# GpSimd takes up node work earlier in the program of a graph layer, and DVE and ACT share the output tiles differently until then

## The reference

```python
deg = jnp.maximum(jnp.zeros((n,), x.dtype).at[dst].add(1.0), 1.0)
edge_weight = (deg[src] * deg[dst]) ** (-DEG_POWER)
edge_msg = jax.nn.relu(edge_attr @ W1e + b1e) @ W2e + b2e
messages = (x[src] + edge_msg) * edge_weight[:, None]
agg = jax.ops.segment_sum(messages, dst, num_segments=n)
combined = (1.0 + gin_eps) * x + agg
h = jax.nn.relu(combined @ W1n + b1n) @ W2n + b2n
out = h + x
out = out * jax.lax.rsqrt(jnp.mean(out * out, axis=-1, keepdims=True) + RMS_EPS) * rms_w
x = _layernorm(x + out, axis=-1)
```

## Time and profile before

| | |
|---|---|
| median of 3 runs | 1333.68 us (1332.87 to 1334.81) |
| the profiled execution | 1332.28 us |
| its span in the profile | 1330.5 us |
| mean granted TensorE clock | 0.970 |
| DVE busy | 1260.0 us, 95% |
| PE busy | 1159.0 us, 87% |
| ACT busy | 1072.8 us, 81% |
| POOL busy | 971.8 us, 73% |

### The profile page before, as it was taken

How to read it: one execution, slowest core, us unless ns; L and a number is a source line. 1 busy time by engine, 2 the same in 40 slices (tenths; PEclk the granted TensorE clock), 3 DMA queues, 4 the chain that set the end, 5 groups by cost and what they waited for, 6 DMA issues and landing times. The chain is left out here.

```text
span 1330.5 us, 32120 instructions
## 1 busy us (share of the span) xinstructions
PE 1159.0 (87%) x7478; PEld 848.1 (64%) x7591; DVE 1260.0 (95%) x4743; ACT 1072.8 (81%) x3857; POOL 971.8 (73%) x1281
## 2 busy tenths in 40 slices
PE   4999729999999999998798888888888888899991
PEld 2555317777777777776576666666666666678771
DVE  5999988999999999999499999999999999899997
ACT  4999505666666666666589999999999999999996
POOL 7777744777777777677777777777777702599896
PEclk9999859999999999999799999999999999999996
DMA  4999964655555555776767888878777665677654
GB/s 123 396 352 396 389 242 111 181 165 171 173 178 177 162 176 172 247 246 249 279 228 260 303 306 298 325 285 306 297 283 282 240 226 196 238 273 278 255 209 184
DMA packets 87132, 327.93 MB, mean 246 GB/s; under 512 B 24657, under 2 KB 27456, under 8 KB 62556
## 3 DMA queue, kind: packets, MB, share of 16 engines
q1 hardware_dynamic: 55832, 256.51, 51.3%
q0 software_dynamic: 29904, 69.48, 17.1%
q10 hardware_dynamic: 1268, 0.54, 0.2%
HBM read 180.14 MB, written 153.95 MB: 251 GB/s over the span
## 5 line engine op out<-in xcount | busy, mean ns | idle before, releaser
L680 POOL DMA_INDIRECT xs<-in_x,src_x x392 | 385.9, 985 | 143.0 <-issue 119.0
L706 POOL DMA_INDIRECT agg_scratch<-staged,sca_i x385 | 381.1, 990 | 121.9 <-issue 113.3
L893 ACT ACTIVATE squares<-res 128x128 f32<-128x128 f32 x784 | 290.1, 604 | 0.5 <-DVE res L1217 0.5
L1433 PE MATMUL bank<-cT,w1n 128*128 128x512 f32 x392 | 215.8, 633 | 68.0 <-ACT cT L875 67.9
L893 ACT ACTIVATION_READ_ACCUMULATOR squares<-res 128x1 f32 x784 | 256.3, 496 | 0.0
L904 ACT ACTIVATE on<-z,offset,rstd 128x128 f32<-128x128 f32 x462 | 255.8, 846 | 0.4 <-DVE offset L1183 0.4
L1410 PEld LDWEIGHTS bank<-w2n,hn 128*128 128x128 f32 x1568 | 206.5, 192 | 70.4 <-issue 64.5
L1410 PE MATMUL bank<-w2n,hn 128*128 128x128 f32 x1568 | 207.3, 275 | 4.2 <-ACT hn L880 0.7
L880 ACT ACTIVATE hn<-bank,b1n_c 128x512 f32<-128x512 f32 x196 | 191.2, 975 | 3.5 <-PE bank L1433 3.5
L1339 PE MATMUL bank<-digits,picks 128*128 128x221 f16 x1568 | 185.2, 260 | 0.0
L875 ACT ACTIVATE cT<-bank 128x512 f32<-128x512 f32 x196 | 172.3, 879 | 8.6 <-PE bank L1426 8.6
(11 more groups left out here) (179 smaller groups left out, 2348.6 us busy)
## 6 DMA issues: line engine op xcount, KB each, us to landing
agg_scratch<-zeros SPq DMA_DIRECT2D x48, 1024.0 KB
xn<-in_x SPq DMA_DIRECT2D x48, 1024.0 KB
out<-on SPq DMA_DIRECT2D x48, 1024.0 KB, 4.5
ag<-agg_scratch SPq DMA_DIRECT2D x47, 1024.0 KB, 7.0
sums_scratch<-sums SPq DMA_DIRECT2D x49, 512.0 KB
staged<-sums_scratch POOLq DMA_DIRECT2D x28, 896.0 KB
highq<-src_key_scratch SPq DMA_DIRECT2D x49, 256.0 KB, 3.7
ea<-in_edge_attr SPq DMA_DIRECT2D x42, 256.0 KB
```

What stands on the lines that cost most here:

```text
L680: pool.indirect_dma_start(out=xs[:, b % XS, j, :], out_offset=None, in_=x, in_offset=bass.IndirectOffsetOnAxis(ap=src_x[:, t:t + 1], axis= ...
L706: pool.indirect_dma_start(out=agg_rows, out_offset=bass.IndirectOffsetOnAxis(ap=sca_i[:, t:t + 1], axis=0), in_=staged[:, k % STAGES, j, : ...
L893: last = act.activation(squares[:, j, :], res[:, s, j, :], ACT.Square, accum_out=ssq[:, v // SPB, s * TB + j:s * TB + j + 1])
L1433: pe.matmul(ps[2 + s][:, :], w1n[:, :], cT[:, s, :], start=True, stop=True).then_inc(hn_done, 1)
```

## The change

GpSimd makes the products from step 104 on (`MIX_ALONE`) and its output tiles from step 88 on (`END_ALONE`), both 128 before. Until step 88 DVE and ACT share the four output tiles 2:2 in even steps and 1:3 in odd ones (`first_ends`), 1:3 before. From step 88 on ACT has tile 3 alone. The written and looped parts move: DVE, ACT and PE now have 0 to 47 written, 48 to 95 looped, 96 to 111 written, 112 to 191 looped; GpSimd begins at 96. In GpSimd's list the output tiles of steps 88 to 91 (n = 106 to 109) stand before the first products, those of step 104 (n = 110).

```diff
-    ALONE = 128
-    assert ALONE % (SPB * XR) == 0 and ALONE <= SPLIT * SPB
+    MIX_ALONE, END_ALONE = 104, 88
+    assert MIX_ALONE <= SPLIT * SPB and END_ALONE <= SPLIT * SPB
...
-            rounds, alone = STEPS // unroll, ALONE // unroll
+            rounds = STEPS // unroll
+            first = min(MIX_ALONE + 6, END_ALONE + 16) // unroll
+            then = -(-max(MIX_ALONE + 7, END_ALONE + 20) // unroll)
...
-            if begin == 0 and alone > 3:
+            if alone_too:
                 written(0, 3 * unroll)
-                looped(3, alone)
-                written(ALONE, ALONE + 2 * unroll)
-            else:
-                written(begin, ALONE + 2 * unroll)
-            looped(alone + 2, rounds)
+                looped(3, first)
+            written(first * unroll, then * unroll)
+            looped(then, rounds)
             written(rounds * unroll, STEPS + tail)
...
+        def mixed_alone(m):
+
+            return below(m, MIX_ALONE)
+
+        def ended_alone(m):
+
+            return below(m, END_ALONE)
+
+        def first_ends(m, v):
+
+            return 2 - v % 2
...
-                if live(m, STEPS) and not solo(m):
+                if live(m, STEPS) and not mixed_alone(m):
                     _, xsl, _, h = place(m, u - 6)
...
-                    if solo(m):
+                    if ended_alone(m):
                         continue
-                    if isinstance(m, int) and m == ALONE:
-                        pool.wait_ge(fin_ready, ALONE)
+                    if isinstance(m, int) and m == END_ALONE:
+                        pool.wait_ge(fin_ready, END_ALONE)
...
-                    share = 3 if solo(m) else 1 if not isinstance(B, int) or B < SPLIT else 2 if B < BLOCKS - 2 else 1 if B < BLOCKS - 1 else 2 if m < STEPS - 1 else 0
+                    share = TB - first_ends(m, v) if ended_alone(m) else 1 if not isinstance(B, int) or B < SPLIT else 2 if B < BLOCKS - 2 else 1 if B < BLOCKS - 1 else 2 if m < STEPS - 1 else 0
...
-                if live(m, STEPS) and solo(m):
+                if live(m, STEPS) and mixed_alone(m):
...
-                if live(m, STEPS) and not solo(m):
-                    dve.wait_ge(xsc_ready, at(m + 1 - ALONE))
+                if live(m, STEPS) and not mixed_alone(m):
+                    dve.wait_ge(xsc_ready, at(m + 1 - MIX_ALONE))
...
-                if live(m, STEPS) and solo(m):
+                if live(m, STEPS) and ended_alone(m):
                     B, o, h = m // SPB, (v // SPB) % OR, (v % SPB) * TB
...
-                    dve.tensor_scalar(on[:, o, h, :], z[:, v, 0, :], neg_mean[:, v // SPB, h:h + 1],
-                                      rstd[:, v // SPB, h:h + 1], ALU.add, ALU.mult).then_inc(fin_ready, 1)
+                    for j in range(first_ends(m, v)):
+                        last = dve.tensor_scalar(on[:, o, h + j, :], z[:, v, j, :], neg_mean[:, v // SPB, h + j:h + j + 1],
+                                                 rstd[:, v // SPB, h + j:h + j + 1], ALU.add, ALU.mult)
+                    last.then_inc(fin_ready, 1)
```

More of the change, by code:

```diff
@@ L411, in run, with run_nodes @@
                 step(n, n % unroll)
-        def run_nodes(eng, step, tail, begin=0):
+        def run_nodes(eng, step, tail, alone_too=True):
             unroll = SPB * XR
-            rounds, alone = STEPS // unroll, ALONE // unroll
+            rounds = STEPS // unroll
+            first = min(MIX_ALONE + 6, END_ALONE + 16) // unroll
+            then = -(-max(MIX_ALONE + 7, END_ALONE + 20) // unroll)
             def written(lo, hi):
@@ L425, in looped, with below @@
                         step(Count(i, unroll, u, lo, hi), u)
-            if begin == 0 and alone > 3:
+            if alone_too:
                 written(0, 3 * unroll)
-                looped(3, alone)
-                written(ALONE, ALONE + 2 * unroll)
-            else:
-                written(begin, ALONE + 2 * unroll)
-            looped(alone + 2, rounds)
+                looped(3, first)
+            written(first * unroll, then * unroll)
+            looped(then, rounds)
             written(rounds * unroll, STEPS + tail)
-        def solo(m):
-            return m < ALONE if isinstance(m, int) else m.below(ALONE)
         def live(n, total):
             return not isinstance(n, int) or 0 <= n < total
+        def below(m, limit):
+            return m < limit if isinstance(m, int) else m.below(limit)
+        def mixed_alone(m):
[4 more added lines that the diff above has]
+            return 2 - v % 2
         def late(B):
@@ L773, in node_step @@
                         last.then_inc(fin_ready, 1)
-            run_nodes(pool, node_step, 15, ALONE)
+            run_nodes(pool, node_step, 15, alone_too=False)
         @block.scalar
```

## The result

The changed kernel takes 1350.13 us, median of 4 runs (1350.01 to 1350.47), against 1333.28 for the kernel before on the same chip: the ratio is 1.0129 (95% interval 1.0117 to 1.0142). It is slower, as forecast, by 17 us instead of 25. All four executions stand within 0.5 us.

The account below looks back on a forecast made before the run. ACT sets 3.616 us a step without GpSimd; mixed, all four engines are full; GpSimd's scatter queue delays the handover. Span 1330.5 + 53.1 - 28.4 = 1355.2, median 1358.4; own range 1349 to 1364, to 1369 with more holes.

Parts of the forecast that it names:

- z of step 104 starts: Handover on DVE: this z waits for GpSimd's scatters, join, output tiles and products, starting at 1079.5 instead of 1026.4, 53.1 us later.
- 88 mixed steps, bare: From the z of step 104 to that of step 192, all steps mixed at 2.832 us each: 249.2 us.
- hole at n=176: Idle stretch where DVE's 16-step loop returns in the mixed stage: 3.3 us, counted once as before, 9.9 more as bound.
- low clock after the wait: PE stands still some 45 us and restarts at the low clock level: 1.5 us lost, bounds 0 and 4.
- from the z of step 192 to the end: Tail of the kernel behind the 88 mixed steps: 21.8 us.
- span: Whole profiled execution: 1330.5 + 53.1 - 28.4 = 1355.2 us.
- GpSimd's release: Join starts 5.3 us after the last scatter, could give back up to 4; it lands in 2.0, bounds 0 and 4.5.
- Rival 2: Mixed loop on DVE: the hole at n=176 repeats at each return, + 9.9 us, 1368; chance 0.15.
- The share: Output tiles 1:3 and 2:2 before the handover: DVE bounds at 3.58 a step; free before the wait, otherwise about 2 us either way.
- Rival 1: Handover: GpSimd free by step 104, no wait worth the name, 18.8 us faster, median 1315; chance 0.04.
- Rival 4: Smaller wait: last scatters and join land at once, no holes, no clock loss, pace 2.809; about 1346; chance 0.05 below 1349.
- Rival 3: Up to step 88, DVE's 44 extra output tiles slow scatters; last one 15 us later, median 1373; chance 0.04.

Follow-up runs that it names:

- experiment 1: Changed kernel with two of every 14 scatters left out (336 instead of 385, output incomplete): 1295.78 us, ratio 0.9722 to the kernel before.
- experiment 5: Changed kernel with products from step 120 and output tiles from step 104, new share: 1314.13 us, ratio 0.9848 to the kernel before.
- experiment 8: Changed kernel with products from step 120 and output tiles from 104, old share 1:3: 1310.95 us, ratio 0.9832 to the kernel before.
- experiment 12: Changed kernel with three DVE output tiles a step and 172 one-column memsets ahead of DVE's node steps: 1355.01 us, ratio 1.0162 to the kernel before.
- experiment 2: Changed kernel with only the new share, GpSimd taking up products and output tiles at 128 as before: 1325.49 us, ratio 0.9942 to the kernel before.
- experiment 3: Changed kernel with products from step 104, output tiles from 128, old share 1:3: 1369.76 us, ratio 1.0276 to the kernel before.
- experiment 4: Changed kernel with products from step 128, output tiles from 88, old share 1:3: 1353.39 us, ratio 1.0153 to the kernel before.
- experiment 6: Changed kernel with products from step 116 and output tiles from step 100, new share: 1319.83 us, ratio 0.9903 to the kernel before.
- experiment 7: Changed kernel with products from step 124 and output tiles from step 108, new share: 1318.67 us, ratio 0.9895 to the kernel before.
- experiment 9: Changed kernel with three output tiles a step on DVE and one on ACT until step 88: 1377.20 us, ratio 1.0331 to the kernel before.
- experiment 10: Changed kernel with two output tiles a step on DVE and two on ACT until step 88: 1353.02 us, ratio 1.0152 to the kernel before.
- experiment 11: Changed kernel with 84 one-column memsets on DVE ahead of its node steps: 1377.91 us, ratio 1.0342 to the kernel before.

## Why the prediction was right

The mechanism held in each step: the change makes DVE wait at the z of step 104 for a GpSimd that is still scattering, and experiment 1 shows that this wait is the whole loss. The size, in span, by the terms of the sum (the terms of the first line add up to 1079.4, not 1079.5):

| term | forecast | measured | difference |
|---|---|---|---|
| z of step 104 starts | 1079.5 | 1076.73 | -2.8 |
| 88 mixed steps, bare | 249.2 | 249.7 | +0.5 |
| hole at n=176 | 3.3 | none | -3.3 |
| low clock after the wait | 1.5 | inside the 249.7, at most 0.5 | -1.5 |
| from the z of step 192 to the end | 21.8 | 21.9 | +0.1 |
| span | 1355.2 | 1348.3 | -6.9 |

The forecast of the median adds 1.4 us more, by which the profiled execution before stood under its median; here the two stand 0.1 us apart. So 1350.1 against 1358.4.

- *GpSimd's release.* The join follows the last scatter 2.08 us later instead of 5.30, since SP's store and loads no longer run beside it. I had named this and left it out of the value. The other runs bear it out, whether DVE waits or not: where SP issued its store and two loads within the 5.5 us up to the last scatter (the kernel before and experiments 1, 5, 8 and 12), the join follows after 5.30 to 6.73 us without work; where SP issued nothing in the 9 us before it (the changed kernel and experiments 2 to 4, 6, 7 and 9 to 11), after 2.08 or 2.09. Landing took 2.10 (I took 2.0).
- *The hole.* I carried the one of before over into a loop that had been moved. It doesn't come with the loop's return as such: the loop now returns four times without one, and in experiment 3, whose loop has the steps 160 to 191 as before but stands elsewhere in the list, the two steps at n=176 take 5.8 us (1276.40 to 1282.18) and not 9.0. In the kernel before, six packets of queue 14 fall between 1233 and 1246, and none between 1220 and 1233. This fits the stretches of experiments 9 and 11, but no run moved the loop of the kernel before alone, so that the hole is the same thing is not shown. Rival 2, which repeated it at each return, was wrong for this kernel; experiments 9 and 11 show that four stretches would have come, of 7 us each and not 3.3, had the loop stood 84 instructions further on. I had no grounds to exclude that, and 1378 lay outside my range: that the time fell inside it is in this respect luck.
- *The clock.* It was down to 0.51 during the wait, close to the lower level of 1.2 GHz, as foreseen. Behind the wait it stayed low for some 4 us: 0.50 from 1077 to 1079, 0.70 on average from 1078 to 1084, 1.00 from 1084 to 1090. So the low clock came as forecast, and only its price was too high: the first four steps behind the wait took 11.7 us (residuals at 1077.34 and 1089.02) against 11.3. The loss is at most half a us.
- *The share.* The pace without GpSimd is 14.33 us for four steps (residuals at 902.61 and 916.94), 3.58 each, as worked out. Alone the share is worth 7 us (experiment 2), not 2: most of what I missed lies between n=135 and n=150. In front of the wait it is worth nothing, as forecast.
- *Rival 1* (no wait) is refuted by the 51.85 us. *Rival 4* (a smaller wait, below 1349) was missed by 1.1 us, and three of its five terms came true: no hole, no loss by the clock worth the name, and 3.2 us less before the join. Its other two didn't: the join still took 2.10 us to land, and the pace was 2.837, not 2.809. *Rival 3* (DVE's tiles hold scatters back) is not seen in this kernel, whose last scatter is 0.45 us late, but see the last section.

## What to carry to other kernels

Before work is moved earlier onto another engine, look in that engine's own rows for when its queue is free, and put the handover there: here 16 steps' difference turned 1.3% lost into 1.5% won, with the same code otherwise. Look at every ring and semaphore through which the old engine meets the new one, since each alone can bring the wait. And when an edit changes the length of an engine's list, look for idle stretches released by nothing at the returns of its later loops: a neutral edit can cost or win 2% there.

## What the runs showed of the hardware

*A loop's return can cost 7 us or nothing.* One body of DVE instructions, 16 steps long, returned four times with idle stretches of 6.2 to 7.2 us or with none, depending on 84 instructions in front of it; moved on by 256 in all it was free again. The Trainium skill, Runtime: NRT & Kernel Launch, section "Instruction fetch mechanics", has instructions fetched in blocks of 256, with room for two, and a branch to a place outside these has to wait for the fetch. The runs agree: the place decides, 256 further on the second loop is alike again, and packets of queue 14 fall around the stretches (20 between 1120 and 1290 in experiment 11, none between 1123 and 1268 in experiment 12). The total of a run says less, since kernels in which DVE has no such stretch have 74 to 90. That a body reaching into a third block is the exact condition was not tried.

*A few scatters take longer than 0.98 us.* GpSimd in the profile with 120/104 and the new share:

```profile
829.84 1.32 POOL L718 DMA_INDIRECT agg_scratch<-staged,sca_i  x1 [0.30 <-issue]
831.46 0.98 POOL L718 DMA_INDIRECT agg_scratch<-staged,sca_i  x1 [0.30 <-DMA agg_scratch<-staged,sca_i]
832.75 1.32 POOL L718 DMA_INDIRECT agg_scratch<-staged,sca_i  x1 [0.30 <-issue]
```

In this profile 45 of 385 scatters take over 1.05 us, ten of them 1.26 to 1.39, and the last starts at 1072.1. In the kernel before and the three runs with the old share it is 10 to 16, and the last starts between 1062.9 and 1063.9. In experiments 2, 5 to 7, 9 and 10, with the new share or more DVE tiles, it is 23 to 45, and the last starts between 1064.6 and 1072.1; experiment 1 has 30 of its 336. But the changed kernel has 11, and experiments 11 and 12, the second with three DVE tiles a step, have 15 and 16. So the number of DVE's tiles doesn't decide it.

The excess of the two long rows, 0.34 us, is about the length of a DVE output tile. The Trainium skill, SBUF — State Buffer, section "SBUF: two separate sides", says that a DVE operation in a mode that uses two ports and GpSimd's writing of descriptors shut each other out. The rows fit that only in part. Between 660 and 1020 in this profile 102 of 257 scatters run beside a DVE output tile; of the 36 long ones there it is 24, which is more than their share, but 12 have none beside them, the one at 829.84 among them. What lengthens these, and why three of the kernels are spared, is open. Whether the long scatters are the reason for the wide range with 120/104 was not tested.
